# The second codes of a quantised MLP stage on GpSimd in place of VectorE, and a new order of VectorE's work

## The reference

```python
def activation_quant(x):
    scale = 127.0 / jnp.clip(jnp.max(jnp.abs(x), axis=-1, keepdims=True), EPS_Q, None)
    return jnp.clip(jnp.round(x * scale), -128, 127) / scale

h = bitlinear(x, norm1_w, w1)      # rmsnorm, activation_quant, product with ternary weights, 256 -> 1024
h = act_scale * jnp.square(jax.nn.relu(h)) + act_bias
y = bitlinear(h, norm2_w, w2)      # the same again, 1024 -> 256
x = x + jnp.tanh(g_ffn[0]) * y     # around it; its input is layernorm(x)
```

## Time and profile before

| | |
|---|---|
| Median of three runs | 4516.61 us |
| Profiled execution | 4504.19 us, span 4502.3 us |
| Mean granted TensorE clock | 0.945 of full |
| Stage B in the span | 859 to 1337 us |
| In these 478 us: PE, PEld busy | 250.0, 178.5 us |
| DVE, ACT, POOL busy | 370.6, 307.0, 0.2 us |
| Mean granted clock in them | 0.74 |

### The profile page before, as it was taken

How to read it: one execution, slowest core, us unless ns; L and a number is a source line. 1 busy time by engine, 2 the same in 40 slices (tenths; PEclk the granted TensorE clock), 3 DMA queues, 4 the chain that set the end, 5 groups by cost and what they waited for, 6 DMA issues and landing times. The chain is left out here.

```text
span 4502.3 us, 85912 instructions
## 1 busy us (share of the span) xinstructions
PE 3970.4 (88%) x29034; PEld 2739.8 (61%) x29034; DVE 2662.7 (59%) x6134; ACT 2006.3 (45%) x3548; POOL 993.3 (22%) x1840
## 2 busy tenths in 40 slices
PE   5999999645558999999979999999899999999999
PEld 3555555334445555555535555555588888888888
DVE  5766666578765777777746666666643333333333
ACT  2555555376653555555535445545432222223222
POOL 2443434000002333333224344444210000000000
PEclk8999999877777999999979999999999999999999
DMA  3000000000000000000000000000120000000000
GB/s 94 12 12 9 12 10 9 25 1 0 0 11 10 10 9 9 9 12 9 3 9 15 19 19 19 19 19 14 45 71 15 29 14 28 14 28 14 24 18 15
DMA packets 79354, 80.32 MB, mean 18 GB/s; under 512 B 4880, under 2 KB 76560, under 8 KB 79248
## 3 DMA queue, kind: packets, MB, share of 16 engines
q1 hardware_dynamic: 79248, 78.91, 5.6%
HBM read 53.73 MB, written 25.17 MB: 18 GB/s over the span
## 5 line engine op out<-in xcount | busy, mean ns | idle before, releaser
L621 DVE TENSOR_REDUCE a_neg_max<-psum 128x2 f32<-128x512 f32 x512 | 328.9, 685 | 192.6 <-PE psum L791 191.3
L1293 DVE TENSOR_REDUCE d_neg_max<-psum 128x2 f32<-128x256 f32 (+1 forms) x512 | 261.3, 553 | 280.6 <-PE psum L1456 278.6
L621 DVE TENSOR_REDUCE c_neg_max<-psum 128x2 f32<-128x512 f32 x512 | 328.6, 684 | 130.4 <-PE psum L791 129.7
L521 ACT ACTIVATE c_exps<-psum 128x512 f32<-128x512 f32 x512 | 277.9, 594 | 243.7 <-PE psum L813 243.6
L521 ACT ACTIVATE a_exps<-psum 128x512 f32<-128x512 f32 x512 | 278.0, 594 | 205.6 <-PE psum L813 205.2
L1196 ACT ACTIVATE d_exps<-psum 128x512 f32<-128x512 f32 (+1 forms) x512 | 223.3, 488 | 285.7 <-PE psum L1483 285.7
L2408 PE MATMUL psum<-e_hidden_l,e_e_l_high 128*128 128x512 f32 x1024 | 321.0, 395 | 0.8 <-POOL e_e_l_low L2170 0.8
L810 PE MATMUL psum<-a_q_by_parity,a_k_stationary 32*128 32x512 f32 x1536 | 270.9, 432 | 23.2 <-ACT a_exps L521 22.5
L791 PE MATMUL psum<-c_k_by_parity,c_q_high_low 32*128 32x512 f32 x1536 | 286.6, 440 | 5.2 <-DVE c_neg_max L621 5.2
L791 PE MATMUL psum<-a_k_by_parity,a_q_high_low 32*128 32x512 f32 x1536 | 267.9, 437 | 9.7 <-DVE a_neg_max L621 9.5
L810 PE MATMUL psum<-c_q_by_parity,c_k_stationary 32*128 32x512 f32 x1536 | 262.7, 436 | 3.8 <-ACT c_exps L521 3.0
(11 more groups left out here) (386 smaller groups left out, 9934.9 us busy)
## 6 DMA issues: line engine op xcount, KB each, us to landing
x_all<-in_x_dram SPq DMA_DIRECT2D x4, 2048.0 KB, 16.0
a_ctx<-in_ctx_t_dram SPq DMA_DIRECT2D x32, 256.0 KB, 2.7
c_ctx<-in_ctx_t_dram SPq DMA_DIRECT2D x32, 256.0 KB, 2.7
x_rows<-d_x SPq DMA_DIRECT2D x32, 256.0 KB, 2.2
out_dram<-d_y SPq DMA_DIRECT2D x32, 256.0 KB, 2.3
e_x<-x_rows SPq DMA_DIRECT2D x16, 512.0 KB, 4.3
e_y<-out_dram SPq DMA_DIRECT2D x16, 512.0 KB, 4.1
out_dram<-e_y SPq DMA_DIRECT2D x16, 512.0 KB, 3.2
```

The lines of the kernel that those rows point to most:

```text
L521: s_.activation(EX[:, t], st_bank[t % 3], ACT.Exp).then_inc(exp_done, 1)
L621: v.tensor_reduce(NM[:, :, t, r, m], sc_bank[u % 3].rearrange("p (e k) -> p e k", e=2), AX.X, ALU.max, negate=True).then_inc(sc_used, 1)
L1293: v.tensor_reduce(NM[:, :, t, r, m], sc_bank[u % 3][:, 0:512 if t else 256].rearrange("p (e k) -> p e k", e=2), AX.X, ALU.max, negate=True ...
```

## The change

GpSimd makes the second codes, four per step, after one instruction that writes a dummy value. It waits for link 9 of the group (`chain_m`) and until all four second codes of the group before have been transposed (`q2t_ready`), and signals `q2_ready` as VectorE did. VectorE loses them, and its order within a step changes:

- `centred` and `centred_max` of a tile stand between and behind `y2` and `y2_max` of a tile;
- links 1 to 4 of the middle chain take turns with links 1 to 4 of the front chain, links 5 to 8 with the four first codes;
- then scale1, link 9, residuals 2 and 3, link 10, statistics 2 and 3. The first codes thus come ahead of link 9 and of the last residuals.

```diff
--- before.py
+++ after.py
@@ -1616,6 +1616,7 @@
             C2 = sb("c2", [P, 2, K])
             Q2 = sb("q2", [P, K, HID1])
             Q2T = sb("q2t", [P, 2, KH2, P], BF16)
+            POOL_DUMP = sb("pool_dump", [P, 1])
             PS = self.PS
             TB = PS[:, 0, :]
             HB = [PS[:, 1 + 2 * n:3 + 2 * n, :] for n in range(2)]
@@ -1664,6 +1665,21 @@
                 g.memset(ONES[:], 1.0).then_inc(ones, 1)
                 g.memset(MINUS_RND[:], -RND).then_inc(ones, 1)
                 pool.wait_ge(ones, 2)
+
+                def second(p, k):
+                    if k == 0:
+                        pool.wait_ge(chain_m, 10 * p + 9)
+                        if known(p, 1):
+                            pool.wait_ge(q2t_ready, 4 * p)
+                        g.tensor_tensor(POOL_DUMP[:], MINUS_RND[:], MINUS_RND[:], ALU.add)
+                    g.tensor_scalar(Q2[:, k], Y2[:, k], S2[:, 7, k:k + 1], RND, ALU.mult, ALU.add).then_inc(q2_ready, 1)
+
+                def step(p, n):
+                    if there(p, 0):
+                        for k in range(K):
+                            second(p, k)
+
+                steps(pool.Fori, step)
 
             @block.scalar
             def _(act):
@@ -1873,12 +1889,6 @@
                             dve.wait_ge(y_used, 4 * (p - 1))
                         m_link(p, 10, v.tensor_scalar(C2[:, n], S2[:, 5], 1.0 / 127.0, WG[:, 0:1], ALU.mult, ALU.mult))
 
-                def second(p, k):
-                    t = 4 * p + k
-                    if known(p, 1):
-                        dve.wait_ge(q2t_ready, 4 * (p - 1) + k + 1)
-                    v.tensor_scalar(Q2[:, k], Y2[:, k], S2[:, 7, k:k + 1], RND, ALU.mult, ALU.add).then_inc(q2_ready, 1)
-
                 def y_update(q, n, k):
                     t = 4 * q + k
                     dve.wait_ge(y_ready, t + 2 - k % 2)
@@ -1898,22 +1908,30 @@
                     for k in range(K):
                         if mid:
                             y2(p, n, k)
+                        if fr:
+                            centred(u, k)
+                        if mid:
                             y2_max(p, k)
+                        if fr:
+                            centred_max(u, k)
                         if up and k == 2:
                             y_update(p - 1, 1 - n, 0)
                             y_update(p - 1, 1 - n, 1)
                         if up and k == 3:
                             y_stats(p - 1, 0)
                             y_stats(p - 1, 1)
+                    for k in range(1, 5):
+                        if mid:
+                            middle(p, n, k)
+                        if fr:
+                            front(u, k)
                     for k in range(K):
                         if mid:
-                            middle(p, n, 2 * k + 1)
+                            middle(p, n, 5 + k)
                         if fr:
-                            centred(u, k)
-                        if mid:
-                            middle(p, n, 2 * k + 2)
-                        if fr:
-                            centred_max(u, k)
+                            quantise(u, k)
+                    if fr:
+                        scale1(u, n)
                     if mid:
                         middle(p, n, 9)
                     if up:
@@ -1923,18 +1941,7 @@
                         middle(p, n, 10)
                     if up:
                         y_stats(p - 1, 2)
-                    for k in range(K):
-                        if mid:
-                            second(p, k)
-                        if fr:
-                            front(u, k + 1)
-                    if fr:
-                        scale1(u, n)
-                    if up:
                         y_stats(p - 1, 3)
-                    if fr:
-                        for k in range(K):
-                            quantise(u, k)
 
                 steps(dve.Fori, step)
                 dve.wait_ge(stats, NT)
```

## The result

The changed kernel takes 4449.54 us (median of four runs, 4439.41 to 4450.62) against 4511.76 us for the kernel before in the same comparison: a ratio of 0.9858, 95% interval 0.9841 to 0.9876. That is 62 us less by the medians and some 64 us by the ratio. The forecast was 4457 us in 4438 to 4490 us. The profiled execution took 4449.63 us, span 4447.8 us, against 4504.19 us.

What follows compares the result with a forecast made beforehand. Engines waiting for each other in a cycle through VectorE's late first codes bound the 27.32 us step; ScalarE's 22.9 us loop would be next. Terms of 2.3, 2.3, 53.0, 0.9 and 0.8 sum to 59.3 us: 4457 us (4438 to 4490).

Steps and rivals of the forecast that it cites:

- step 0: First step of the quantised stage, 19.47 us: 2.3 us less, as the squares that step 1 waits for end at 927.53.
- step 1: Second step of the quantised stage: from 25.21 us to ScalarE's 22.9 us, 2.3 us less.
- steps 2 to 13: The twelve regular steps of the quantised stage: from 27.32 to 22.9 us each, 53.0 us less in all.
- last group: End of the quantised stage: second codes no longer stand behind 1.49 us of residuals and statistics, 0.8 us less.
- ScalarE's loop as the floor: Regular steps: with first codes always ready in PSUM, ScalarE's own loop of 22.9 us sets the step.
- VectorE's work: VectorE per step: 23.98 us less 2.7 for second codes and 0.8 for the order, 20.5 us (19.8 to 21.3).
- The stall at the residuals: VectorE's wait for the second products in each step: 0.4 to 0.8 us remains of 3.34 us.
- The second codes on GpSimd: Four codes per step at 1.12 us each, taken from line 438; GpSimd then needs 4.8 us per step.
- rival C: Codes cost 3.15 us each on GpSimd, as line 397 suggests; kernel slower than before, 4530 to 4564 us; chance 0.09.
- The clock: TensorE's granted clock stays low in the first part of each step, as some 4 us of idle time remains.
- Rival D: Early transposes keep TensorE's clock at 2.4 GHz, ScalarE's gaps shrink some 1.5 us; about 4440 us; chance 0.07.
- The upper bound for y2: Next step's first y2 on VectorE waits for all four GpSimd codes: loop at most 23.2 us (22.5 to 24.0).

Runs made afterwards that it cites:

- the two padded kernels: Changed kernel plus one instruction per step: a 1.06 us square on ScalarE, 23.78 us per regular step; or a 1.2 us maximum on VectorE, 22.76 us.

## Why the prediction was right

By its own terms, in the stage:

| Term | Forecast, us | Measured, us |
|---|---|---|
| step 0 | 2.3 | 19.47 - 17.22 = 2.25 |
| step 1 | 2.3 | 25.21 - 23.15 = 2.06 |
| steps 2 to 13 | 12 x 4.42 = 53.0 | 327.83 - 273.49 = 54.3 |
| step 14 | 0.9 | 23.85 - 23.24 = 0.61 |
| last group | 0.8 | 30.66 - 30.25 = 0.41 |
| sum | 59.3 | 59.7 |

- *ScalarE's loop as the floor.* Right: 22.9 us forecast, 22.79 us measured, and the two padded kernels show that it is ScalarE's loop and not VectorE's work.
- *VectorE's work.* 20.5 us were worked out; the step that begins at 1084.60 is 23.22 us long, with 2.21 us of idle time at its end and 0.67 us at the residuals, so it is 20.34 us. The 23.98 us that the prediction calls busy hold some 2 us of short waits within the chains: 2.15 us per step before and 1.02 us after. So the order saved 1.1 us of them where I had taken 0.8, and 0.31 us was lost at link 10.
- *The stall at the residuals.* 0.4 to 0.8 us forecast; 0.12 to 0.75 us in five of the twelve regular steps, nothing in the others.
- *The second codes on GpSimd.* Right in taking line 438's 1.12 us: 1.10 us each, 4.7 us from link 9 to the last one. The Trainium skill (GPSIMD Engine Reference, "3.1 Elementwise — side-by-side cycle accounting") gives about 2.6 cycles per element, an estimated 2.2 us, but it says there that the figure is that of a tensor_tensor with two inputs. A code reads one tile, so the figure was no argument for rival C. The trace says half of 2.2 us with two operations, and more, 2.83 us, with one.
- *The clock.* Kept low at the start of steps, as forecast; it rises later in one step of three than in the others, which costs that step 0.6 us. Rival D's price was about right: the steps with 20 matmuls in time took 21.2 us. Its condition did not come about by itself.
- *The upper bound for y2.* Too high. I let it wait for all four codes; it waits for one instruction at a time. In the changed kernel y2 lost a turn in step 1 (2.05 us at 924.78); in the regular steps all 48 took 1.27 or 1.28 us. The sum did not rest on it.
- *Rival C.* Its condition was wrong: it was to decide from 2.15 us per code, and 2.83 us per code left the step as it was.
- *What I did not see.* The prediction lists the 2.7 us that leave VectorE as the first part of the change and never asks what the order would bring without it. By its own numbers, 20.5 + 2.7 is 23.2 us and after the first slack hardly more than ScalarE's 22.9 us. The runs give the whole gain to the order, and to the move of the codes nothing (-1.7 us in the stage, by one trace of each), because the time that it frees is waiting time. So the total is right and its division between the two parts of the change is not: the 2.7 us stand in VectorE's sum, and that sum did not decide.

The time as a whole fell by 54.6 us in the profiled executions, 5.1 us less than the stage: the stage's first step began 3.2 us earlier, and everything behind the stage took 3173.2 us in place of 3164.9 us. The change touches nothing there, and the kernels here differ by as much in those stages without a pattern (3158.8 to 3186.9 us). That the median came within 8 us of the forecast is in that sense partly luck; the stage is the part that was worked out.

## What to carry to other kernels

Before work is moved off the busiest engine, look for who waits for that work and when: here the first codes stood behind work that nobody was in a hurry for, and changing the order on VectorE gave all of the gain without moving anything to another engine. Work out each engine's own loop with its inputs always ready; the largest of these, not the busiest engine's sum, is what a better order can reach. Work given to GpSimd also takes turns away from VectorE: put beside it what was not held here (residuals that read PSUM, the statistics, the maxima, which took 1.21 us beside codes too), and keep chains of tiny instructions out of its time.

## What the runs showed of the hardware

- GpSimd's tensor_scalar and some of VectorE's instructions exclude each other and alternate, one instruction each, when both have work: a y2 of 1.27 us took 2.13 us and a code of 1.12 us took 2.09 us, side by side. A VectorE instruction of 4 values took up to 1.08 us in place of 0.17 us. Reciprocals (0.18 us), maxima (1.21 us) and statistics (0.43 us) were not held. The Trainium skill (SBUF — State Buffer, "Who interferes with whom") states the exclusion, for the whole of an instruction and for one with two SBUF inputs as well; the trace agrees for codes with two operations, where the turns are seen in y2, which has two such inputs, and differs for those with one, which are the next point.
- On GpSimd a tensor_scalar of 128x1024 float32 values takes 1.10 us with two operations (multiply, add) and 2.83 us with one (multiply). In the second case a VectorE instruction is held only in the first 1.1 us or so: the mean square ended 1.13 us after the start of a code, and a y2 begun 1.05 us after it took its usual 1.27 us. That the instruction has read its data by then would explain it; this was not tested.
- Twenty matmuls whose results nobody reads hold TensorE at its 2.4 GHz level through what had been an idle time (granted clock 1.00), here in every second step. The step is then 1.6 us shorter where they end in time and 0.4 us longer where they end 2 us or more after ScalarE's first copy.
